# A gather ring with a lead that shrinks toward the end of a layer, and with the whole ring as lead: two graph layers on one core

## The reference

```python
h = relu(layernorm(x))
neigh = segment_sum(h[src], dst)                       # layer 0: sum over incoming edges
x = x + relu(relu(((1 + eps) * h + neigh) @ W1 + b1) @ W2 + b2)
h = relu(layernorm(x))
out = h @ w_self.T                                     # layer 1: a matrix for each of 16 relations
for e in edges: out[src[e]] += h[dst[e]] @ weights[edge_type[e]]
x = x + out
```

## Time and profile before

| | us |
|---|---|
| median of three runs | 1488.99 (1488.04 to 1506.56) |
| the profiled execution | 1480.42 |
| its span, from first to last instruction | 1478.6 |
| start of sort 2's groups on TensorE | 516 |
| layer 0's last matmul | 781 |
| GpSimd goes on with the last layer | 954 |
| GpSimd's last gather is issued | 1457 |
| the last chunk's matmul ends | 1468 |

### The profile page before, as it was taken

One profiled execution on the slowest core, in us unless ns is written; L12 is line 12 of the kernel. 1 busy time (PEld: TensorE's weight loads), 2 busy tenths in 40 slices (PEclk: granted clock), 3 DMA queues, 4 the chain that ended last, 5 costly groups with the idle time before them and its releaser, 6 DMA issues.

```text
span 1478.6 us, 12987 instructions
## 1 busy us (share of the span) xinstructions
PE 900.4 (61%) x3719; PEld 538.7 (36%) x3719; DVE 725.7 (49%) x2168; ACT 374.1 (25%) x945; POOL 827.2 (56%) x833
## 2 busy tenths in 40 slices
PE   5533953699450088989878826936755554544535
PEld 2311430254130055657554402524533433333324
DVE  8822884586385786889865302313432222222212
ACT  8111520464220075777743302100000000000000
POOL 0375347687437266655560472166666666666663
PEclk8565975699585589999988957957876566565667
DMA  3522323234322034332332735711111111111114
GB/s 83 156 76 67 85 67 106 54 116 121 83 63 78 26 87 115 98 112 83 108 68 85 251 81 160 225 45 47 47 48 47 46 47 44 46 47 45 46 47 69
DMA packets 50307, 122.86 MB, mean 83 GB/s; under 512 B 16156, under 2 KB 27021, under 8 KB 47487
## 3 DMA queue, kind: packets, MB, share of 16 engines
q0 software_dynamic: 33088, 67.82, 18.4%
q1 hardware_dynamic: 16844, 52.62, 11.4%
q10 hardware_dynamic: 308, 1.60, 0.4%
HBM read 71.86 MB, written 50.10 MB: 82 GB/s over the span
## 4 chain that ended last, share of the span: by engine, by line
PE 20%; POOL 18%; DVE 12%; issue 12%; another core or an unknown queue 8%; DMA 1%; ACT 1%; POOLq 0%; DVEq 0%; ACTq 0%
POOL gathered L419 18%; PE ps L981 5%; PE ps L1063 4%; PE ps L954 3%; PE ps L956 3%; DVE scratch L733 3%; PE ps L985 3%; DVE spare L678 2%; DVE node_hot L796 1%; DVE spare L628 1%; DVE place_val_a L728 1%; DVE chunk_f L683 1%; DVE place_hot L723 1%; DMA gathered<-z_table,row_of 1%
## 5 line engine op out<-in xcount | busy, mean ns | idle before, releaser
L419 POOL DMA_INDIRECT gathered<-h_table,row_of x416 | 436.2, 1049 | 334.4 <-issue 116.4
L419 POOL DMA_INDIRECT gathered<-z_table,row_of x410 | 388.4, 947 | 295.8 <-issue 117.8
L981 PE MATMUL ps<-node_hot,gathered 128*128 128x250 f32 x820 | 277.4, 493 | 235.2 <-issue 141.9
L985 PE MATMUL ps<-node_hot,gathered 128*128 128x506 bf16 (+1 forms) x1248 | 248.1, 347 | 139.1 <-DVE node_hot L796 79.8
L796 DVE TENSOR_SCALAR node_hot<-iota_f,key_of 128x250 f32<-128x250 f32 x410 | 140.1, 375 | 373.7 <-remote 169.8
L981 PEld LDWEIGHTS ps<-node_hot,gathered 128*128 128x128 f32 x820 | 188.3, 245 | 323.7 <-issue 301.8
L985 PEld LDWEIGHTS ps<-node_hot,gathered 128*128 128x128 bf16 x1248 | 124.8, 102 | 250.4 <-issue 182.8
L494 ACT ACTIVATE place_val_b<-place_hot,code_b 125x128 f16<-125x128 f16 x400 | 173.3, 518 | 164.6 <-DVE place_hot L723 146.3
L486 ACT ACTIVATE scratch<-scratch,code_b 125x208 f16<-125x208 f16 (+1 forms) x328 | 116.5, 431 | 252.9 <-issue 144.8
L954 PE MATMUL ps<-scratch,place_val_a 125*128 125x410 f16 x400 | 142.2, 356 | 11.3 <-DVE scratch L733 9.9
L956 PE MATMUL ps<-scratch,place_val_b 125*128 125x410 f16 x400 | 140.0, 350 | 1.5 <-issue 1.5
(11 more groups left out here) (167 smaller groups left out, 519.1 us busy)
## 6 DMA issues: line engine op xcount, KB each, us to landing
z_table<-spare SPq DMA_DIRECT2D x50, 448.0 KB
z_table<-zeros_z SPq DMA_DIRECT2D x19, 896.0 KB
gathered<-h_table,row_of POOLq DMA_INDIRECT x416
gathered<-z_table,row_of POOLq DMA_INDIRECT x410
z_table<-spare SPq DMA_DIRECT2D x50, 52.0 KB
z_table<-zeros_z SPq DMA_DIRECT2D x19, 104.0 KB
out<-x_sb SPq DMA_DIRECT2D x6, 224.0 KB
h_table<-gathered SPq DMA_DIRECT2D x1, 1092.0 KB
```

Source lines behind the costliest of these rows:

```text
L419: pool.indirect_dma_start(place if s == LAST else place.rearrange("p j d -> p (j d)"), None, z_table if s == LAST else h_table, bass.Indir ...
L981: last = T.matmul(psf[:, bass.ds(offs[i], WIDE[s])], rows, node_hot_of[s][:, k % HOTS[s], :], start=False, stop=False, skip_group_check=True)
L985: last = T.matmul(psf[:, bass.ds(offs[i], WIDE[s])], rows[:, part, :], node_hot_of[s][:, k % HOTS[s], :], start=False, stop=False, skip_gr ...
```

## The change

GpSimd's wait ahead of a group now always lets it lead by the whole ring, 13 groups in layer 0 and 15 in the last layer. The function `lag_of` and its two constants go. No instruction is added or taken away; only the values for which GpSimd waits at line 416 get smaller, for groups 27 to 51 of sort 2 and 16 to 81 of the last layer.

```diff
-GROUPS_L = (sum(GROUPS[:LAST]), GROUPS[LAST])
-LEAST_LAG = 4
...
-        def lag_of(s, g):
-
-            l, gg = int(s == LAST), (GROUPS_BEFORE[s] if s < LAST else 0) + g
-            left = GROUPS_L[0] - gg if l == 0 else 2 * RING_L[1] - (gg - RING_L[1])
-            return min(RING_L[l], max(LEAST_LAG + l, left // 2))
-
...
                 for g in range(GROUPS[s]):
-                    used = used_up_to(s, g, lag_of(s, g))
+                    used = used_up_to(s, g, RING_L[s == LAST])
```

## The result

The changed kernel takes 1523.57 us (median of four runs, 1521.1 to 1525.83) against 1488.51 us (1481.14 to 1506.56) before: a ratio of 1.0238, 95% interval 1.0185 to 1.029. A second measurement on another occasion gave 1.0287 (1.0201 to 1.0372). Ratios compare fast runs only: executions more than 1.5% above the fastest of their kernel are left out of them. It is slower, by 35 us at these medians; whether by more than 2% the first interval leaves open, while the second lies just above that.

The account below looks back on a forecast made before the run. The order of waits was taken to bound the kernel, with increments late during unbroken gathers. Layer 0's +14 and the last layer's +18 gave +32 us on 1489, 1521, put at 1519; range 1483 to 1550.

Parts of the forecast that it names:

- What bounds the kernel: Whole kernel: the order of waits decides; the last layer hangs mostly on GpSimd's gathers, with 60 us of waits among them.
- Late increments: Three places: while GpSimd gathers without a long pause, TensorE's increments get through at one in 3 to 5 us.
- Sort 2, term +20 with a lower bound of 0: Sort 2 from group 27: GpSimd ends near 755, TensorE at 772 in place of 752; 20 us later at most.
- The end of layer 0, term -6: End of layer 0: the last gathers land early, so TensorE's wait of 5.87 us goes; 6 us back.
- The last layer, term +18: Last layer: GpSimd ends almost as before, but TensorE has 35 to 65 chunks left; 11 to 27 us later.
- The idle lead: Rival, chance 0.23: increments are equally late at any lead; only layer 0's 6 us are gained, 1483 us.
- One of the two terms only: Rival, chance 0.17: only sort 2's or only the last layer's slowdown comes, +12 to +18 us, 1501 to 1507.
- The faster case: Rival, chance 0.05: the short lead causes GpSimd's last-layer waits; the full ring removes 60 us of them, 1433 us.
- The much slower one: Rival, chance 0.05: the trickle worsens with longer unbroken runs; two more long stretches, one per layer, 1559 us and above.

Follow-up runs that it names:

- e7: Kernel before, but VectorE makes only the first 9 of the last layer's 410 one-hot matrices, so TensorE waits there only for landed gathers; 1480.08 us, one run.
- e5: Kernel before with a lead of 4 groups all through layer 0, the last layer unchanged; ratio 1.0018.
- e2: Kernel before with the whole ring as lead in the last layer only, layer 0 keeping its shrinking lead; ratio 1.0136.
- e9: e5 with ten of GpSimd's dense-stage groups each waiting for three more halves of z tiles from TensorE; 1427.09 us, ratio 0.9707.
- e11: Kernel before with ten of GpSimd's dense-stage groups each waiting for three more halves of z tiles from TensorE; 1461.43 us, ratio 0.9858.
- e10: Changed kernel, with GpSimd doing five fills, some 3 us, ahead of every second group in the last layer; 1557.93 us, one run.
- e8: Kernel before, with GpSimd doing five small fills, some 3 us, ahead of every second group in sorts 0 and 1; 1486.95 us, one run.

## Why the prediction was right, point by point

The forecast was 1519 us against a measured 1524, +30 against +35, in the right direction. That it lies so close is in part luck: the traces differ by 45 us where the sum of the terms was 32, and the timed halves add up to 1.6%, 24 us. Point by point:

- *What bounds the kernel.* GpSimd's waits in the last layer were read as TensorE's progress coming late, not as the lead being too short. The trace after bears it out: 66 us of waits both with a lead of 15 groups and with one of 5, and 502 and 504 us for the 355 gathers. This reading decided between slower and faster.
- *Late increments.* Right, but not the whole of it: the bursts in e7 and in the kernel before show increments that come long after their matmuls, and single matmuls 2.1 to 2.8 us apart in e7 show TensorE's instructions held up too. Which of the two is at work changes no number of the sum. A fifth of TensorE's increments cured nothing, and in the last layer of e7 VectorE sends almost none. So the bug that the Trainium skill warns of ("VectorE: DVE Perf Modes", section "The TRN2 errata") isn't borne out, as far as the rate of these two engines' increments goes; those that come with the gathers' landings weren't varied by themselves.
- *Sort 2, term +20 with a lower bound of 0.* GpSimd ended at 754 (755 forecast). TensorE was done with group 46 at 788 and not at 772: the term measured 35 us between these two traces (28 between the averages of all), since the pace was 6.0 us a group and not the 5.55 of the stretch before 603. The term was also bounded from the wrong side; its upper bound was no bound.
- *The end of layer 0, term -6.* Right in kind: no wait for a landing was left. From group 46 to the last matmul it took 17 us in place of 27.6, 10 us less. Both together +24 where +14 was forecast; by timed runs the half in layer 0 is under 10 us. The traces say that the term was too small, the timed runs that it was too large, and which of them holds is open. That a lead of 13 groups sets the pace of a stretch, on which the term rests, is in doubt too, since a lead of 4 gave the same pace (e5).
- *The last layer, term +18.* GpSimd's last gather 502 us after its restart (503 before), 62 chunks left where 35 to 65 were given, 0.46 us each where 0.54 was taken, some 30 us of work behind the last gather less the 10 that were there: +20, and 19 for the whole layer. In e2, the half alone, +1.4%, 20 us. This term is the one that is shown in traces and timed runs alike.
- *The rivals.* The idle lead (1483) fell with sort 2's pace and with the row of 122 matmuls at the end. *One of the two terms only* (1501 to 1507) lies below the whole, whose interval starts at 1.0185 (1516), but the timed half in layer 0 is what it describes. In e7 single matmuls stand up to 2.8 us apart while GpSimd gathers. By the Trainium skill, "SBUF — State Buffer", section "Who interferes with whom", TensorE never waits for another engine at that memory's ports; TensorE is held up all the same here, and whether at these ports or elsewhere no run shows. The faster case fell with GpSimd's 66 us of waits. The much slower one didn't come (its 40 us had no working: two more standstills of 44.52 us would be 89); a full ring presumably ends each unbroken run before it gets that long, but no run tests it.
- *What was overlooked.* The dense stage. The stage takes 175 us in the kernel before and 177 in the changed one, and 146 with paced gathers (e9). The pattern was to be seen in the trace of before.

## What to carry to other kernels

How far an engine that issues gathers may run ahead isn't free here: it is worth what the others can use before the end, and TensorE and its increments fall behind in long unbroken runs of gathers. What is gathered ahead is paid back at the end, when the gatherer is done and a whole ring of work is left to engines that stood still before. Where rows show an engine's idle time ending each time another one pauses, pace that one by the progress of the first, also in stages where the two have nothing to do with each other (e9, e11). A small constant lead isn't that by itself (e5).

## What the runs showed of the hardware

- While GpSimd issues indirect gathers at one in 1.25 us without a break, TensorE's increments reach the other engines at one chunk in 3 to 5.6 us (5.60 us apart, five in a row, in e7), and its matmuls can come 2.1 to 2.8 us apart. Within 1 to 6 us of GpSimd's standstill the increments in arrears arrive 0.04 us apart, and matmuls go on at 0.42 to 0.93 us a chunk. Slow stretches were seen in both layers and in the dense stage, where TensorE had no dependence on the gathers (24.52 us idle, until a copy that was waiting for its increment).
- Runs of 10 gathers, each followed by 3 us in which GpSimd fills a tile, kept TensorE's unexplained idle time at 4 us over a whole layer (e10). Runs of 8 with the same fills in sorts 0 and 1 broke up a standstill of 44.5 us but hardly shortened the stage, 199 us in place of 204 (e8).
- What in the gathers does it (descriptors, their transfers, or something else) no run here tells apart, and neither what the smallest pause is. Left open. A load of instructions did not end the stall in the dense stage: the queues that carry such loads moved no packet from 840 to 932.
